# Attention of a decoder layer: queries normalised, turned and projected one quarter earlier, and stacked ahead of the keys

## The chip, the cores and the metric

The kernel runs on one core of one Trainium2 chip, as a single launch. The metric is the device time of that launch in microseconds (us). The engines are named as in the profile: PE is TensorE (PEld its weight loads), DVE is VectorE, ACT is ScalarE, POOL is GpSimd, SP is SyncE, which here only issues DMAs (SPq is its queue).

## What is computed

One decoder layer on x of shape (32, 100, 256), in fp32: a recurrent token mixer, a cross attention of 16 heads against a context of 361 keys with 192 channels, and a mixture of 8 experts of which 2 are taken per token. The change touches the second stage alone:

```python
    def _L0_xattn_ref(query, key_value, Wq, bq, Wk, bk, Wv, bv, Wo, bo):
        q = (query @ Wq + bq).reshape(B, Nq, H, D).transpose(0, 2, 1, 3)
        k = (key_value @ Wk + bk).reshape(B, Nkv, H, D).transpose(0, 2, 1, 3)
        v = (key_value @ Wv + bv).reshape(B, Nkv, H, D).transpose(0, 2, 1, 3)
        attn = jnp.einsum('bhqd,bhkd->bhqk', q, k) * scale
        attn = jnp.clip(attn, -CLAMP, CLAMP)
        attn = jax.nn.softmax(attn, axis=-1)
        x = jnp.einsum('bhqk,bhkd->bqhd', attn, v).reshape(B, Nq, Cq)
        return x @ Wo + bo
    x = x + _L0_attn_ref(_layernorm(x, axis=-1), ...)
    x = x + _L0_xattn_ref(_layernorm(x, axis=-1), ctx_768, ...)
    x = x + _L0_ffn_ref(_layernorm(x, axis=-1), ...)
```

## The kernel before

The three stages run one after the other: the mixer, the attention, the experts. Every engine has its own program, written out by hand, and runs it strictly in that order; semaphores tie the programs together. Nothing reorders them.

**The loop of the attention.** `every_batch` writes out 32 bodies, one for each batch b. A body has four quarters t = 0 to 3; a quarter handles four of the 16 heads. In quarter t PE computes, in this order: half of the scores of the next quarter (`scores`, L1551, into `bank_s`), the transposed scores of this quarter in three pieces (`scores_t`, L1561, into `bank_st`), the weighted sum of the quarter before (`weigh`, L1581), the other half of the next quarter's scores, and last `shift` (L1570), which subtracts each row's maximum by a matmul with a diagonal of maxima. The scores of the next batch's first quarter are thus computed in quarter 3: this is where PE first needs the next batch's queries and keys.

**Around it.** DVE takes the maxima of `bank_s` (L1357), writes them negated (L1362), and clips `bank_st` (L1368). POOL builds the diagonal from the maxima (`diag`, L1086, tile `neg_diag`); `shift` of quarter t waits for `diag` of quarter t. ACT takes the exponentials after `shift` (`exps`, L1231).

**Queries and keys.** The scores are taken in bf16 with each fp32 number split in three parts. ACT rounds to the high part (L1210 for a half of the keys, L1225 for all queries), and POOL computes the middle and the low part (`split_k`, L1067 to L1071, once for each half; `split_q`, L1076 to L1080). SP then copies the parts of 16 channels each into `k_st` and `q_st`, six slots of 16 partitions on top of each other (`stack`, L965): 12 DMAs for the keys and 12 for the queries of a batch, waiting for each part before its copies. `k_st` and `q_st` hold three batches.

The queries of batch b + 2 are prepared in body b: POOL computes the norm's factors (`norm`, L1047 to L1051), ACT applies them in quarter 1 (L1264), PE turns the result at the end of quarter 2 (`turn`, L1522), ACT copies it (`turned`, L1214), PE projects it at the end of quarter 3 (`queries`, L1529), and ACT adds the bias and rounds (L1221, L1225). The keys of b + 2 are projected in quarters 2 and 3 (L1514). POOL splits the second half of the keys and the queries at the start of body b + 1, ahead of that body's `diag` of quarter 1.

**What POOL does besides.** In even bodies from b = 4 on it also sends the routed rows of two earlier batches to HBM (`tag`, `count_on`, and four indirect DMAs, `send`, L1133: two ahead of `diag(b, 3)`, one behind it, one ahead of `diag(b + 1, 0)`). In odd bodies it has `route_pair` (L1094 to L1104) ahead of `diag(b, 3)`. `norm3` (L1056 to L1060) belongs to the third stage's layer norm; ACT's `row` (L1272) and PE's turn of it (L1610, in quarter 0) wait for it.

## Time and profile before

| | us |
|---|---|
| median of 3 runs | 1618.37 |
| lowest, highest | 1614.95, 1623.78 |
| profiled execution, its own time | 1619.98 |
| its span in the trace | 1618.1 |

The trace covers the profiled execution; 1.9 us lie around its span. The mixer takes the first 494 us, the attention runs from there to about 1249 us, and the experts from then on. The attention's loop starts at 526.0 us with the first scores and takes its batches at 22.3 us each. The profile shows for each engine its instructions in order of time, how long it sat idle before one, and what ended that idle time (the releaser, behind "<-"). [...]

### The profile page before, as it was taken

The page shows a single profiled execution, that of the slowest core. Times are in us where ns is not written, and L with a number is a line of the kernel's source. Part 1 is how long each engine was busy: PE and PEld are TensorE (multiplying, and loading weights), DVE is VectorE, ACT ScalarE, POOL GpSimd, SP SyncE. Part 2 cuts the span into 40 slices and gives each one's busy share as a digit, 9 for nine tenths or more (in the row PEclk, how much of TensorE's full clock was granted, in tenths as well). Part 3 has the DMA queues.
Part 4 walks back from the last instruction along what each step waited for, and adds up shares of the span by engine and source line. Part 5 has one row for each costly group of instructions (what it writes and reads, how often), then busy time and mean ns, then how long its engine had stood idle before and what let it go on. Part 6 is the DMA issues. An engine that isn't in the chain of part 4 may idle for free. (4 is left out here: it accounts for less than half of the span.)

```text
span 1618.1 us, 31781 instructions
## 1 busy us (share of the span) xinstructions
PE 1365.9 (84%) x9914; PEld 916.8 (57%) x9915; DVE 988.9 (61%) x2297; ACT 578.7 (36%) x1420; POOL 801.1 (50%) x1138
## 2 busy tenths in 40 slices
PE   4788778778746899988898888998886699999996
PEld 2455555545534566666666666666653366666664
DVE  2687987797740777877777777787875122222221
ACT  1333323323312455554444545445543121222221
POOL 4234642463343557776676676776764122222222
PEclk9899999999965999999999999999996799999999
DMA  4991000000004655555555565655551132222222
GB/s 147 322 321 39 1 1 1 0 0 1 1 0 79 92 92 111 118 111 106 111 106 113 107 111 88 116 116 110 112 100 53 40 46 46 46 45 44 44 46 23
DMA packets 180331, 128.03 MB, mean 79 GB/s; under 512 B 69010, under 2 KB 173090, under 8 KB 180194
## 3 DMA queue, kind: packets, MB, share of 16 engines
q1 hardware_dynamic: 167890, 112.23, 32.8%
q0 software_dynamic: 12304, 14.10, 5.8%
q8 instruction: 70, 1.15, 0.4%
q14 instruction: 67, 0.55, 0.1%
HBM read 36.10 MB, written 44.83 MB: 50 GB/s over the span
## 5 line engine op out<-in xcount | busy, mean ns | idle before, releaser
L1357 DVE TENSOR_REDUCE neg_raw<-bank_s 100x2 f32<-100x722 f32 x256 | 230.8, 902 | 95.0 <-PE bank_s L1551 82.8
L1231 ACT ACTIVATE prob<-bank_st 120x400 f32<-120x400 f32 (+1 forms) x384 | 166.4, 513 | 220.3 <-PE bank_st L1570 213.6
L1892 POOL DMA_INDIRECT out<-result,target x57 | 88.2, 1547 | 266.9 <-DVE result L1866 263.9
L1368 DVE TENSOR_SCALAR bank_st<-bank_st 120x400 f32<-120x400 f32 (+1 forms) x384 | 196.6, 573 | 0.0
L751 PE MATMUL bank_l<-q_heads,k 128*100 128x192 f32 (+4 forms) x512 | 126.9, 390 | 62.0 <-DVE attn L565 49.9
L1551 PE MATMUL bank_s<-k_st,q_st 96*128 96x361 bf16 x512 | 129.7, 336 | 56.5 <-DMA q_st<-q_part 53.7
L1877 DVE TENSOR_TENSOR hidden<-silu,ebank_v 128x512 f32<-128x512 f32 x57 | 39.2, 688 | 196.9 <-PE ebank_v L1801 196.9
L751 PEld LDWEIGHTS bank_l<-q_heads,k 128*100 128x100 f32 x512 | 82.8, 180 | 113.0 <-DVE attn L565 43.5
L399 ACT ACTIVATE q_heads<-q 32x192 f32<-32x192 f32 (+3 forms) x168 | 62.1, 369 | 226.3 <-DVE q L524 220.7
L1086 POOL TENSOR_TENSOR neg_diag<-xident_b,neg_max 100x400 bf16<-100x400 bf16 x128 | 109.3, 854 | 60.4 <-DVE neg_max L1362 57.4
L1514 PE MATMUL bank_m<-kv,xw_k 96*128 96x361 f32 x256 | 107.8, 551 | 10.9 <-DMA kv<-in_ctx_t 10.2
L1801 PE MATMUL ebank_g<-expert_w,rows_t 128*128 x228 | 109.9, 605 | 1.2 <-DVE rows_t L1857 0.8
L275 POOL TENSOR_TENSOR mixed<-part,xn_t 128x400 f32<-128x400 f32 x80 | 78.9, 1012 | 63.5 <-DVE part L441 63.5
L1561 PE MATMUL bank_st<-q_st,k_st 96*128 96x100 bf16 x1536 | 105.2, 211 | 4.2 <-ACT prob L1231 0.3
L1820 PE MATMUL ebank_y<-residual,hidden_t 128*128 x456 | 108.0, 380 | 0.9 <-ACT hidden_t L1848 0.9
L1801 PE MATMUL ebank_v<-expert_w,rows_t 128*128 x228 | 108.0, 596 | 0.0
L1561 PEld LDWEIGHTS bank_st<-q_st,k_st 96*128 96x128 bf16 x1536 | 84.6, 100 | 38.1 <-ACT prob L1231 25.4
L1848 ACT ACTIVATE hidden_t<-ebank_h 128x512 f32<-128x512 f32 x57 | 34.0, 597 | 198.1 <-PE ebank_h L1811 198.1
L1539 PE MATMUL bank_v<-xw_v,kv 96*120 96x256 f32 (+1 forms) x384 | 98.5, 394 | 1.4 <-ACT xval L1249 0.7
L1581 PE MATMUL bank_o<-prob,xval 120*32 120x100 f32 (+1 forms) x3072 | 98.1, 263 | 0.5 <-ACT prob L1231 0.5
L281 POOL TENSOR_TENSOR gn_rstd<-gn_mv,eps 100x16 f32<-100x16 f32 x8 | 2.4, 300 | 183.6 <-DVE gn_mv L578 183.6
L1570 PE MATMUL bank_st<-neg_diag,xones_b 100*128 100x400 bf16 x384 | 89.9, 342 | 2.2 <-POOL neg_diag L1086 1.8
(207 smaller groups left out, 2734.0 us busy)
## 6 DMA issues: line engine op xcount, KB each, us to landing
k_st<-k_part SPq DMA_DIRECT2D x384, 90.2 KB
slot_rows<-empty SPq DMA_DIRECT2D x9, 2967.0 KB, 26.0
q_st<-q_part SPq DMA_DIRECT2D x384, 25.0 KB
kv<-in_ctx_t SPq DMA_DIRECT2D x32, 270.8 KB
expert_w<-in_w SPq DMA_DIRECT2D x16, 512.0 KB, 3.9
rows<-slot_rows SPq DMA_DIRECT2D x57, 129.0 KB
residual<-in_w SPq DMA_DIRECT2D x16, 256.0 KB, 4.4
residual<-in_x SPq DMA_DIRECT2D x8, 400.0 KB
```

The source lines that it names most:

```text
L751: pe.matmul(bank[0:T, at:at + RH * cols], k[:, p, j, 0:T], q_heads[:, lv % 2, :, j, 0:cols], start=True, stop=True).then_inc(level_summed, 1)
L1086: pool.tensor_tensor(neg_diag[:, t % 2], ident_b[:].unsqueeze(1).to_broadcast([T, 4, T]), neg_max[:, 4 * t:4 * t + 4].unsqueeze(2).to_broa ...
L1231: act.activation(prob[0:KEYS[c], t % 2, c], bank_st[c][0:KEYS[c], 0:4 * T], ACT.Exp).then_inc(exp_done, 1)
L1357: dve.tensor_reduce(neg_raw[:, h:h + 2], bank_s[0:T, :, 0:S], AX.X, ALU.max, negate=True).then_inc(max_done, 1)
L1368: dve.tensor_scalar(tile, tile, CLAMP, -CLAMP, ALU.min, ALU.max).then_inc(clipped, 1)
L1514: mm = pe.matmul(bank_m[:, 0:S], w_k[:, i, c * 128:(c + 1) * 128], kv[:, p, i], start=(i == 0), stop=(i == 1))
L1539: mm = pe.matmul(bank_v[0:KEYS[c], (c % 2) * D:(c % 2 + 1) * D], kv[:, p, i, KEY0[c]:KEY0[c] + KEYS[c]], w_v[:, i], start=(i == 0), stop=( ...
L1551: mm = pe.matmul(bank_s[0:WIDE, i, 0:S], q_st[:, r, h * T:h * T + WIDE], k_st[:, r, h * S:(h + 1) * S], start=True, stop=True)
L1561: mm = pe.matmul(bank_st[c][0:WIDE, j * T:(j + 1) * T], k_st[:, r, at:at + WIDE], q_st[:, r, h * T:(h + 1) * T], start=(j == 0), stop=Fals ...
L1581: mm = pe.matmul(bank_o[32 * j:32 * j + 32, t * T:(t + 1) * T], val[0:KEYS[c], p, c, 17 * (4 * t + j):17 * (4 * t + j) + 32], prob[0:KEYS[ ...
L1801: mm = pe.matmul(dst[:], rows_t[:, u, c], w1_of[:, bass.ds(expert, 1), c, half * F:(half + 1) * F].rearrange("p o f -> p (o f)"), start=(c ...
L1820: mm = pe.matmul(bank_y[:, 0:D], hidden_t[:, u, f], w2_of[:, bass.ds(expert, 1), f].rearrange("p o d -> p (o d)"), start=(f == 0), stop=(f ...
```

## The change

In the steady bodies of the attention the chain that prepares the queries of batch b + 2 moves one quarter forward on every engine, and SP copies the queries of a batch before its keys. The instructions and their shapes are the same, and so is their number.

```diff
@@ stack(b, r), on SP
                 until(st_summed, 12 * (b - 2))
                 until(s_summed, 8 * (b - 2))
-                for c in range(CC):
-                    until(k_high, CC * b + c + 1)
-                    spread(k_st, k_part, (0, 2, 5), 0, c, k_stacked)
-                    until(k_mid, CC * b + c + 1)
-                    spread(k_st, k_part, (1, 4), 1, c, k_stacked)
-                    until(k_low, CC * b + c + 1)
-                    spread(k_st, k_part, (3,), 2, c, k_stacked)
                 until(q_high, b + 1)
...
                     spread(q_st, q_part, (5,), 2, c, q_stacked)
+                for c in range(CC):
+                    until(k_high, CC * b + c + 1)
+                    spread(k_st, k_part, (0, 2, 5), 0, c, k_stacked)
+                    until(k_mid, CC * b + c + 1)
+                    spread(k_st, k_part, (1, 4), 1, c, k_stacked)
+                    until(k_low, CC * b + c + 1)
+                    spread(k_st, k_part, (3,), 2, c, k_stacked)
@@ body, on POOL
+                if more_than(b, 2):
+                    norm(b + 2)
                 if more_than(b, 1):
                     split_k(b + 1, 1)
-                    split_q(b + 1)
+                if b == 0:
+                    split_q(1)
                 diag(b, 1)
-                if more_than(b, 2):
-                    norm(b + 2)
@@
                 diag(b, 3)
+                if more_than(b, 2):
+                    split_q(b + 2)
                 if sends:
                     send(h, hp, 1, 0)
@@ body, on ACT
                     exps(4 * b + t, t)
                     if t == 1 and more_than(b, 2):
-                        norm(b + 2)
+                        turned(b + 2)
...
+                    if t == 0 and more_than(b, 2):
+                        norm(b + 2)
                     if more_than(b, 2) and t >= 2:
                         keys(b + 2, t - 2)
                     if more_than(b, 2) and t == 2:
-                        turned(b + 2)
-                    if more_than(b, 2) and t == 3:
                         queries(b + 2)
@@ body, on PE
+                    if more2 and t == 1:
+                        turn(b + 2)
                     if more2 and t == 2:
-                        turn(b + 2)
-                    if more2 and t == 3:
                         queries(b + 2)
```

**POOL, an even body with sends.** From the send behind `diag(b, 3)` to `diag(b + 1, 0)`, before:

```order
L1133 DMA slot_rows<-row,slots 26496x258
L1056 TENSOR_TENSOR moment<-moment,xeps 100x1
L1058 TENSOR_TENSOR moment<-moment,xpower 100x1
L1060 TENSOR_SCALAR moment<-moment 100x1
L1067 TENSOR_TENSOR kr<-kf,k_part 128x361
L1068 TENSOR_TENSOR k_part<-kf,k_part 128x361
L1071 TENSOR_TENSOR k_part<-kr,k_part 128x361
L1133 DMA slot_rows<-row,slots 26496x258
L1086 TENSOR_TENSOR neg_diag<-xident_b,neg_max 100x400
```

and with the change:

```order
L1076 TENSOR_TENSOR qr<-qf,q_part 128x200
L1077 TENSOR_TENSOR q_part<-qf,q_part 128x200
L1080 TENSOR_TENSOR q_part<-qr,q_part 128x200
L1133 DMA slot_rows<-row,slots 26496x258
L1056 TENSOR_TENSOR moment<-moment,xeps 100x1
L1058 TENSOR_TENSOR moment<-moment,xpower 100x1
L1060 TENSOR_SCALAR moment<-moment 100x1
L1067 TENSOR_TENSOR kr<-kf,k_part 128x361
L1068 TENSOR_TENSOR k_part<-kf,k_part 128x361
L1071 TENSOR_TENSOR k_part<-kr,k_part 128x361
L1133 DMA slot_rows<-row,slots 26496x258
L1086 TENSOR_TENSOR neg_diag<-xident_b,neg_max 100x400
```

The three operations of `split_q` moved from behind `diag(b + 1, 0)` to well ahead of it, and they wait there for ACT's rounded queries.

**PE, from the end of quarter 2 to the start of the next body's quarter 0.** Before:

```order
L1570 MATMUL bank_st<-neg_diag,xones_b 128x400 x3
L1522 MATMUL bank_v<-xident,xxn 128x100 x2
L1551 MATMUL bank_s<-k_st,q_st 128x361 x2
L1561 MATMUL bank_st<-q_st,k_st 128x100 x12
L1581 MATMUL bank_o<-prob,xval 32x100 x12
L1551 MATMUL bank_s<-k_st,q_st 128x361 x2
L1514 MATMUL bank_m<-kv,xw_k 128x361 x2
L1570 MATMUL bank_st<-neg_diag,xones_b 128x400 x3
L1529 MATMUL bank_v<-xxn_t,xw_q 128x100 x4
L1551 MATMUL bank_s<-k_st,q_st 128x361 x2
L1561 MATMUL bank_st<-q_st,k_st 128x100 x12
```

and with the change (its lines stand 3 further down in the file):

```order
L1573 MATMUL bank_st<-neg_diag,xones_b 128x400 x3
L1532 MATMUL bank_v<-xxn_t,xw_q 128x100 x4
L1554 MATMUL bank_s<-k_st,q_st 128x361 x2
L1564 MATMUL bank_st<-q_st,k_st 128x100 x12
L1584 MATMUL bank_o<-prob,xval 32x100 x12
L1554 MATMUL bank_s<-k_st,q_st 128x361 x2
L1517 MATMUL bank_m<-kv,xw_k 128x361 x2
L1573 MATMUL bank_st<-neg_diag,xones_b 128x400 x3
L1554 MATMUL bank_s<-k_st,q_st 128x361 x2
L1564 MATMUL bank_st<-q_st,k_st 128x100 x12
```

The projection of the queries now stands ahead of the next batch's first scores, and nothing stands any more between `shift` of quarter 3 and the next body.

## Rows read from the trace of the kernel before

**Rows 1.** Who waited for whom: engine, line, releaser: total us, times, longest.

```profile
PE bank_s L1551 <- DMA q_st<-q_part: 53.7, 30, 2.9
PE bank_st L1570 <- POOL neg_diag L1086: 1.8, 1, 1.8
```

**Rows 2.** Busy time by stretch: bounds, length, engines' busy us, clock, DMA, GB/s.

```profile
608.30:1187.98 579.68, 516.88 (x5721) 365.57 (x5722) 440.83 (x949) 293.73 (x796) 413.47 (x693) 0.96 0.57 109
...
807.80:813.90 6.10, 6.04 (x55) 4.09 (x56) 4.62 (x9) 1.76 (x6) 5.35 (x9) 0.72 0.46 117
```

**Rows 3.** PE's timeline, even body 16: start, us, line, operation [idle before <-releaser].

```profile
896.42 0.67 PE L1570 MATMUL bank_st<-neg_diag,xones_b 100*128 100x400 bf16 x3
...
898.66 0.47 PE L1551 MATMUL bank_s<-k_st,q_st 96*128 96x361 bf16 x2 [1.39 <-DMA q_st<-q_part]
...
902.29 1.03 PE L1529 MATMUL bank_v<-xxn_t,xw_q 128*128 128x100 f32 x8
...
907.21 0.67 PE L1570 MATMUL bank_st<-neg_diag,xones_b 100*128 100x400 bf16 x3
```

**Rows 4.** PE's timeline, quarter 3 of even body 12, released after a wait.

```profile
807.86 0.47 PE L1551 MATMUL bank_s<-k_st,q_st 96*128 96x361 bf16 x2 [1.47 <-DMA q_st<-q_part]
...
813.13 1.03 PE L1529 MATMUL bank_v<-xxn_t,xw_q 128*128 128x100 f32 x8
```

**Rows 5.** SP's queue: the 12 copies of a batch's queries, in two bodies.

```profile
798.32 7.65 SPq L965 DMA_DIRECT2D q_st<-q_part  x12
...
820.50 8.54 SPq L965 DMA_DIRECT2D q_st<-q_part  x12
```

**Rows 6.** ACT's timeline in the same even body: quarter 2 behind the exponentials, then quarter 3.

```profile
898.51 0.58 ACT L1204 ACTIVATE kf<-bank_m,xb_k 128x361 f32<-128x361 f32 x1
898.96 0.36 ACT L1214 ACTIVATE xxn_t<-bank_v 128x200 f32<-128x200 f32 x1
...
904.26 0.59 ACT L1221 ACTIVATE qf<-bank_v,xb_q 128x100 f32<-128x100 f32 x2
904.89 0.37 ACT L1225 ACTIVATE q_part<-qf 128x200 bf16<-128x200 f32 x1
```

**Rows 7.** POOL's timeline around the same body, splitting queries and sending rows.

```profile
887.08 0.56 POOL L1076 TENSOR_TENSOR qr<-qf,q_part 128x200 f32<-128x200 f32 x1
...
888.83 0.86 POOL L1086 TENSOR_TENSOR neg_diag<-xident_b,neg_max 100x400 bf16<-100x400 bf16 x1
...
898.45 0.85 POOL L1086 TENSOR_TENSOR neg_diag<-xident_b,neg_max 100x400 bf16<-100x400 bf16 x1 [1.88 <-DVE neg_max L1362]
...
905.74 0.86 POOL L1086 TENSOR_TENSOR neg_diag<-xident_b,neg_max 100x400 bf16<-100x400 bf16 x1
```

**Rows 8.** PE's timeline, odd body 13's quarter 3 to even body 14's quarter 2.

```profile
830.69 0.47 PE L1551 MATMUL bank_s<-k_st,q_st 96*128 96x361 bf16 x2 [2.15 <-DMA q_st<-q_part]
831.00 0.70 PE L1561 MATMUL bank_st<-q_st,k_st 96*128 96x100 bf16 x12
...
834.33 1.03 PE L1529 MATMUL bank_v<-xxn_t,xw_q 128*128 128x100 f32 x8
835.20 0.47 PE L1551 MATMUL bank_s<-k_st,q_st 96*128 96x361 bf16 x2
...
839.89 0.67 PE L1570 MATMUL bank_st<-neg_diag,xones_b 100*128 100x400 bf16 x3
...
849.75 0.67 PE L1570 MATMUL bank_st<-neg_diag,xones_b 100*128 100x400 bf16 x3
```

**Rows 9.** PE's timeline, body 0: transposed scores with little ahead of them.

```profile
544.03 1.08 PE L1561 MATMUL bank_st<-q_st,k_st 96*128 96x100 bf16 x12
```

**Rows 10.** The loop's start: ACT's first rounded queries, PE's first scores.

```profile
512.20 0.37 ACT L1225 ACTIVATE q_part<-qf 128x200 bf16<-128x200 f32 x1
...
525.98 0.47 PE L1551 MATMUL bank_s<-k_st,q_st 96*128 96x361 bf16 x2
```

**Rows 11.** PE's timeline, body 30: the loop's last wait for a stack.

```profile
1210.73 0.47 PE L1551 MATMUL bank_s<-k_st,q_st 96*128 96x361 bf16 x2 [2.04 <-DMA q_st<-q_part]
```

## The prediction, made before the change was run

> **What bounds the kernel now.** I read the table of waits first. PE waits 30 times, 53.7 us in all, for a landing of queries ahead of L1551 [rows 1]: once a body, at the start of quarter 3, where the next batch's first scores begin. Next, the busy time by stretch: over 26 bodies PE is busy 516.9 of 579.7 us (89%), POOL 413.5 (71%), DVE 440.8 (76%) [rows 2]. A body takes 579.7 / 26 = 22.3 us, a pair of an even and an odd body 44.6 us; 26 bodies x 1.8 us of this wait are most of PE's idle time. Last, the timelines around the wait. [...]
>
> The wait is SP's. Twelve copies take 7.65 us to issue even when nothing holds them up [rows 5], 0.64 us each; the last ends at 805.97 and PE is released at 807.86 [rows 4], 1.9 us later.
>
> **The change, step by step.** All times are counted from the start of `shift` of quarter 2, S.
>
> SP. The high parts of the queries now open the stack. Behind the exponentials of quarter 2 the keys' bias starts at S + 2.09 (898.51 - 896.42) [rows 3, 6], the next operation 0.45 after that (898.96); the queries' bias and rounding take 0.63 (904.26 to 904.89) + 0.37 [rows 6]. So the high parts are ready at S + 3.55. 24 copies at 0.64 are 15.3 us; in another body 12 took 8.54 instead of 7.65 [rows 5], so I add 0.9; with 1.9 for landing all is there at S + 21.7. PE wants it one body later at S' + 1.4 (the two start-ups of `shift`, 0.51, and of the projection, 0.87, from 834.33 to 835.20 [rows 8]). With a body of 20.3 us or more the wait at quarter 3 is gone. SP no longer pauses between the pieces, since each part is ready before it is asked for. The landing of the larger last piece (keys, 90 KB against 25 KB) is seen in no row; I take the queries' 1.9 us, from 1.9 to 3.1 for the range. [...]
>
> PE. The projection (0.87) leaves quarter 3 and the turn (0.34) quarter 2; they stand one quarter earlier. Their work is unchanged, but the projection was cover: behind `shift` of quarter 3 the transposed scores must now wait for ACT's exponentials. Where only the turn stood there, the 12 took 1.08 instead of 0.70 us (544.03 against 831.00) [rows 8, 9]; with nothing there I take 0.5 us, from 0.4 to 0.9.
>
> POOL is where I expect the gain to be lost. In an even body with sends, it goes from the end of the diagonal of quarter 3 (898.45 + 0.85 = 899.30) to the start of the next body's first diagonal (905.74) without a pause: a send, `norm3`, `split_k`, a send, 6.44 us [rows 7]. PE uses that diagonal at 907.21, 0.6 us after its end [rows 3, 7]. There is hardly slack even now. The change puts `split_q` ahead of all of it, 1.75 us (887.08 to 888.83) [rows 7], and it has to wait until S + 3.55 for ACT, 0.65 us after POOL came free. The diagonal then ends at 3.6 + 1.75 + 6.44 + 0.86 = S + 12.7. PE would like to have it at 1.4 (its scores begin) + 3.63 (quarter 3 without the projection, 898.66 to 902.29) + 0.5 + 4.05 (907.21 - 902.29 - 0.87) [rows 3] = S + 9.6. **A new wait of 3.1 us for `neg_diag` in every second body.** Until now PE waited for it once in the whole run, 1.8 us [rows 1]. Behind the waiting `shift` stand the routing, the next scores and, on ACT, the exponentials; nothing of them can pass.
>
> The odd body: no sends, but `diag` of quarter 3 stands behind `route_pair`. Its own end is late, yet 1.75 + about 1.2 + 2.7 + 0.85 us later PE is only about at its `shift`: from S it needs 0.51 + 0.87 + 3.64 + 0.5 + 4.69 (835.20 to 839.89) = 10.2 us [rows 8]. I count no wait there, 0.5 at the most.
>
> The sum for a pair. From the even body's S to the odd body's first `shift`: 12.7 us (before: 907.21 - 896.42 = 10.8 in this body [rows 3]; with a low stretch in it 12.3). From first `shift` to S inside a body: 9.86 (839.89 to 849.75) [rows 8] + 0.34 for the turn = 10.2, twice. From the odd body's S to the next first `shift`: 10.2. Together 43.3 us, against 44.6: 1.3 us less a pair, at the upper clock throughout. Thirteen pairs have sends: -16.9 us.
>
> The clock. Before, the low stretches came behind waits of 1.4 to 2.9 us, behind some and not others (807.86 yes, 830.69 no, by the time that quarter 3 took [rows 4, 8]), roughly once a pair. The new wait is longer but comes half as often. I take a low stretch behind every second one: 6.5 x 1.6 = +10.4. The bounds are 0 and 13 x 1.6 = +20.8. [...]
>
> The ends. At the start the first copies of keys no longer run ahead: SP begins with the queries at 512.6 [rows 10], issues 24 copies in 15.7 us and PE begins at about 530.1 instead of 525.98: +4.1. Bodies 1 to 3 have no sends, so their waits really go (about 1.2 a body and a low stretch): -4.7. Body 30 has no `split_q`, so its wait of 2.04 us [rows 11] goes and a low stretch with it (1.6), less 1.1 of new stalls behind exponentials: -2.5. These three make -3.1.
>
> Sum: -16.9 + 10.4 - 3.1 = -9.6 us. The profiled execution took 1620.0, so it would take 1610.4; it lies 1.6 above the median, and the forecast is 1618.4 - 9.6 = **1609 us**.
>
> **The rivals.**
> *No wait for POOL.* If the sends or the splits give way and PE gets its diagonal in time, a body is bounded by PE and the stack, 20.4 to 20.8 us: 26 x 1.8 = 47 us less, 1570 us. [...] Against it: the 6.44 us without a pause [rows 7]. 10%.
> *The clock falls behind every new wait.* The gain of 1.3 is less than the 1.6 of a low stretch: 13 x 0.3 = +4, less 3.1: 1619 us. 20%.
> *Slower.* The wait for `neg_diag` is so long that a low stretch lasts twice as long (3.2 us). It decides from 1.3 us of low-clock loss per pair on; 13 x (3.2 - 1.3) - 3 = +22: 1640 us. For it: PE idles 3.1 us within 9, longer than any wait now (2.9 [rows 1]). Against it: by then the next bodies have slack again. 12%.
> *The change doesn't do what it says:* the last keys land as late as the queries did, because SP's queue still ends late; the same wait under another name beside POOL's: 1622 us. Against it are the pauses that SP loses. 8%.
>
> **How the numbers follow.** My forecast, a wait for POOL with the clock falling behind some of its waits, has 50%, with 1599 to 1617 as its own range (clock bounds, 12.5 to 12.9 for POOL's chain, 0.4 to 0.9 for ACT's). A measurement of this kernel tells about 0.5%, 8 us, from no change: below 1610.3 faster, above 1626.5 slower. Faster takes 0.34 of my forecast and the first rival: 0.44. Slower: the third rival and a little of the rest, 0.14. Same: 0.42. The range reaches over the second and fourth rival and leaves out the first and most of the third: 1589 to 1631.
>
> **What would show it.** Right: the wait for `q_st` at L1554 nearly gone from the table; a new entry of PE for `neg_diag` (L1573 for L1086) of 25 to 45 us in 12 to 14 waits, all at quarter 0 of odd bodies; SP copying without pauses; transposed scores at 1.1 instead of 0.7 us in quarter 0; the first scores at about 530 us. Wrong: waits for `k_st` at quarter 3 (SP is the bound), no wait for `neg_diag` (POOL had room), or ACT's `row` (L1273) reached so late that PE stops at its turn (L1613) for more than a microsecond. The clock's share, 0.96 over the 26 bodies now [rows 2], tells the rivals apart: 0.97 or more gives the lower end of the forecast, 0.95 or less the slower case.

## The result and the profile after

The changed kernel takes 1663.35 us (median of 4 runs, 1651.83 to 1670.75), the kernel before beside it 1617.84 (4 runs). The ratio is 1.027, with a 95% interval of 1.0193 to 1.0347. The forecast was 1609, the range 1589 to 1631: the kernel became slower, and by more than any of the rivals allowed (1640 at the most). One execution of a kernel of the experiments (e5) took 2315.28 us at a granted clock of 0.556, and no median or ratio below counts it.

The profiled execution is the slowest of the four (1670.75 us). The first lines of its page, and the granted clock by slices:

```profile
span 1668.9 us, 31781 instructions
## 1 busy us (share of the span) xinstructions
PE 1406.0 (84%) x9914; PEld 937.4 (56%) x9915; DVE 984.4 (59%) x2297; ACT 591.1 (35%) x1420; POOL 800.8 (48%) x1138
...
PEclk9899999999775898997899889989998699999999
```

The same 26 bodies as in [rows 2], the busy time by stretch, first after, then before. The stretch runs from the first scores of batch 4, in quarter 3 of body 3, to those of batch 30. The columns are the bounds, the length, the busy time of PE, PEld, DVE, ACT and POOL (instructions), the granted clock, the share of the DMA engines and GB/s:

```profile
627.05:1237.86 610.81, 554.15 (x5722) 385.43 (x5721) 436.48 (x950) 304.15 (x794) 412.33 (x689) 0.91 0.65 102
```

```profile
608.32:1187.94 579.62, 516.84 (x5720) 365.51 (x5721) 440.83 (x949) 293.71 (x796) 413.43 (x692) 0.96 0.57 109
```

The two spans differ by 1668.9 - 1618.1 = 50.8 us. The bounds of these lines split it: bodies 4 to 29, counted so, begin 627.05 - 608.32 = **18.7** us later, take 610.8 - 579.6 = **31.2** longer, and what follows takes 431.0 instead of 430.2, **0.9** more.

The 31.2 us are no idle time. PE's idle time in the stretch went from 579.62 - 516.84 = 62.8 to 610.81 - 554.15 = 56.7 us: down by 6.1. Its busy time, for the same 5720 matmuls, went up by 37.3. The clock column gives the reason, 0.91 instead of 0.96.
```profile
903.84:907.26 3.42, 3.37 (x33) 2.48 (x33) 3.13 (x7) 0.39 (x1) 3.01 (x4) 0.50 1.14 120
920.90:927.73 6.83, 6.83 (x43) 4.92 (x44) 4.01 (x8) 1.52 (x5) 6.37 (x11) 0.50 0.31 66
```

Where the waits went, from the table of waits (engine, line, releaser: total us, times, longest):

```profile
PE bank_s L1554 <- DMA k_st<-k_part: 24.3, 8, 8.0
PE bank_st L1573 <- POOL neg_diag L1086: 21.7, 14, 1.8
PE bank_m L1627 <- ACT kf L1207: 14.0, 14, 1.1
PE bank_m L1613 <- ACT kf L1207: 8.5, 10, 0.9
```

Before, behind the start, PE waited for `kf` only at `count`:

```profile
PE bank_m L1624 <- ACT kf L1204: 4.9, 14, 0.4
```

The 53.7 us for `q_st` of [rows 1] are gone. There came the wait for `neg_diag` that was foretold (13 of the 14 stand in odd bodies; the one in body 31 was there before), and one that was named only as a sign of being wrong: PE waits for ACT's `kf` (the keys' bias, counted by `k_done`), in even bodies at `count` (L1627; 4.9 us in 14 before), in odd ones at `turn3` (L1613; none before). Both, in PE's timeline of odd body 15 and even body 16 (start, us, line, operation, idle time before it and releaser):

```profile
889.55 0.67 PE L1573 MATMUL bank_st<-neg_diag,xones_b 100*128 100x400 bf16 x3
...
895.00 1.15 PE L1564 MATMUL bank_st<-q_st,k_st 96*128 96x100 bf16 x12
...
898.11 0.36 PE L1613 MATMUL bank_m<-xident,row 100*128 100x100 f32 x2 [0.90 <-ACT kf L1207]
898.31 1.91 PE L1542 MATMUL bank_v<-xw_v,kv 96*121 96x256 f32 x8
901.77 0.68 PE L1573 MATMUL bank_st<-neg_diag,xones_b 100*128 100x400 bf16 x3 [1.55 <-POOL neg_diag L1086]
...
904.89 1.23 PE L1584 MATMUL bank_o<-prob,xval 121*32 121x100 f32 x24
...
920.82 0.41 PE L1627 MATMUL bank_m<-pairs,before 100*100 100x16 f32 x2 [1.05 <-ACT kf L1207]
...
923.56 3.66 PE L1542 MATMUL bank_v<-xw_v,kv 96*121 96x256 f32 x8
```

In one pair PE stops three times, 0.90, 1.55 and 1.05 us, where before it stopped twice for the stack. Behind the last two the clock fell: the 24 matmuls of L1584 take 1.23 us at 904.89 (0.72 at the upper clock, as in e9's rows below), and the values of L1542 3.66 at 923.56 instead of 1.91 at 898.31.

POOL's timeline from quarter 3 of even body 14 to that odd body's first diagonal shows why `neg_diag` is late, and why `kf` is:

```profile
890.38 0.85 POOL L1086 TENSOR_TENSOR neg_diag<-xident_b,neg_max 100x400 bf16<-100x400 bf16 x1 [1.60 <-DVE neg_max L1365]
892.61 0.56 POOL L1076 TENSOR_TENSOR qr<-qf,q_part 128x200 f32<-128x200 f32 x1 [1.38 <-ACT q_part L1228]
...
896.62 0.26 POOL L1060 TENSOR_SCALAR moment<-moment 100x1 f32<-100x1 f32 x1
...
900.86 0.86 POOL L1086 TENSOR_TENSOR neg_diag<-xident_b,neg_max 100x400 bf16<-100x400 bf16 x1
```

From the `shift` of quarter 2 at 889.55, POOL waits for the rounded queries until 3.06 us, and the next diagonal ends at 901.72, 12.17 us; the forecast said 12.7. `norm3` (`moment`) now stands behind the split. Its result releases ACT's `row`, and `kf` stands behind `row` on ACT.

The start. SP's queue, then ACT's timeline, then PE's:

```profile
512.11 7.80 SPq L965 DMA_DIRECT2D q_st<-q_part  x12
520.43 7.71 SPq L965 DMA_DIRECT2D k_st<-k_part  x12
...
535.53 10.88 SPq L965 DMA_DIRECT2D q_st<-q_part  x12
546.53 8.99 SPq L965 DMA_DIRECT2D k_st<-k_part  x12
```

```profile
533.09 0.51 ACT L1213 ACTIVATE k_part<-kf 128x361 bf16<-128x361 f32 x1 [11.60 <-DMA k_st<-k_part]
```

```profile
533.05 0.78 PE L1554 MATMUL bank_s<-k_st,q_st 96*128 96x361 bf16 x2 [7.62 <-DMA k_st<-k_part]
...
560.32 0.78 PE L1554 MATMUL bank_s<-k_st,q_st 96*128 96x361 bf16 x2 [8.02 <-DMA k_st<-k_part]
```

The first scores come at 533.05, 7.1 us later than in [rows 10] (4.1 were expected). Worse is body 0. `k_part` is one buffer: by the program ACT may round the keys of batch 1 only when all key copies of batch 0 have landed, and these now go last. So ACT stands 11.60 us, the queries of batch 1, which stand behind on ACT, are rounded after it, and SP begins the second stack at 535.53. Quarter 3 of body 0 waits 8.02 us for it.

Landing. SP issued the last key copy of the first stack at 520.43 + 7.71 = 528.14, and PE was released at 533.05, 4.9 us later. The forecast took 1.9. The busy time by stretch in bodies 11 and 12 (columns as above; the last but one is the DMA engines' share, which counts a transfer where it starts and so can pass 1), first while SP issues twelve key copies, then from the last issue to PE's scores:

```profile
805.99:813.72 7.73, 7.05 (x62) 5.05 (x63) 4.33 (x11) 3.40 (x10) 6.29 (x11) 0.78 0.96 120
813.72:818.98 5.26, 5.26 (x61) 3.95 (x60) 4.28 (x9) 2.10 (x6) 0.00 (x0) 1.00 1.16 157
```

Before, over the query copies of [rows 5] at 820.50:

```profile
820.50:829.03 8.53, 7.77 (x91) 5.11 (x88) 7.20 (x16) 3.49 (x10) 3.98 (x8) 1.00 0.49 53
```

Twelve key copies in a row keep the DMA engines at a share of 0.96, and at 1.16 for 5 us after SP has done: they are issued as fast as they are moved, and a backlog remains. Wherever PE waited for `k_st` in this kernel and those below whose key copies go last, it was released 3.0 to 6.5 us after SP's last copy, mostly 4 to 6 (without a wait its scores began as early as 2.7 us after it); before, behind the queries' copies, PE was released after 1.5 to 2.1. There SP paused between the pieces of the keys (11.63 to 12.20 us for twelve copies, at 808.75 and 786.01, against 7.73 here), and the small copies of the queries ended the stack at a share of 0.49.

### The profile page after: what moved, and what is told of

Read it like the earlier page. It is cut to its first block and busy times, and to the rows that moved or that the text cites. A ratio compares the mean times of both kernels' runs of the same rounds, so it can differ in the third digit from the quotient of the medians.

```text
span 1668.9 us, 31781 instructions
## 1 busy us (share of the span) xinstructions
PE 1406.0 (84%) x9914; PEld 937.4 (56%) x9915; DVE 984.4 (59%) x2297; ACT 591.1 (35%) x1420; POOL 800.8 (48%) x1138
## 3 DMA queue, kind: packets, MB, share of 16 engines
q8 instruction: 70, 1.15, 0.3%
## 5 line engine op out<-in xcount | busy, mean ns | idle before, releaser
L1554 PE MATMUL bank_s<-k_st,q_st 96*128 96x361 bf16 x512 | 134.1, 346 | 27.7 <-DMA k_st<-k_part 24.3
L1542 PE MATMUL bank_v<-xw_v,kv 96*120 96x256 f32 (+1 forms) x384 | 120.9, 462 | 1.4 <-ACT xval L1252 0.8
L1564 PE MATMUL bank_st<-q_st,k_st 96*128 96x100 bf16 x1536 | 113.4, 215 | 4.7 <-ACT prob L1234 0.7
L1573 PE MATMUL bank_st<-neg_diag,xones_b 100*128 100x400 bf16 x384 | 91.4, 345 | 22.5 <-POOL neg_diag L1086 21.7
L1584 PE MATMUL bank_o<-prob,xval 120*32 120x100 f32 (+1 forms) x3072 | 105.0, 276 | 0.5 <-ACT prob L1234 0.5
L1517 PE MATMUL bank_m<-kv,xw_k 96*128 96x361 f32 x256 | 95.4, 497 | 11.0 <-DMA kv<-in_ctx_t 10.3
L1542 PEld LDWEIGHTS bank_v<-xw_v,kv 96*120 96x120 f32 (+1 forms) x384 | 85.9, 234 | 20.2 <-issue 2.1
```

Of the source, the lines that this page charges most:

```text
L1517: mm = pe.matmul(bank_m[:, 0:S], w_k[:, i, c * 128:(c + 1) * 128], kv[:, p, i], start=(i == 0), stop=(i == 1))
L1542: mm = pe.matmul(bank_v[0:KEYS[c], (c % 2) * D:(c % 2 + 1) * D], kv[:, p, i, KEY0[c]:KEY0[c] + KEYS[c]], w_v[:, i], start=(i == 0), stop=( ...
L1554: mm = pe.matmul(bank_s[0:WIDE, i, 0:S], q_st[:, r, h * T:h * T + WIDE], k_st[:, r, h * S:(h + 1) * S], start=True, stop=True)
L1564: mm = pe.matmul(bank_st[c][0:WIDE, j * T:(j + 1) * T], k_st[:, r, at:at + WIDE], q_st[:, r, h * T:(h + 1) * T], start=(j == 0), stop=Fals ...
L1584: mm = pe.matmul(bank_o[32 * j:32 * j + 32, t * T:(t + 1) * T], val[0:KEYS[c], p, c, 17 * (4 * t + j):17 * (4 * t + j) + 32], prob[0:KEYS[ ...
```

## The experiments

Each kernel ran beside the kernel before, three rounds and more. "26 bodies" is bodies 4 to 29, counted as above, in the profiled execution, "low" the time at a clock of 0.50 in them, "stack" PE's waits ahead of the first scores of a batch in the whole run (total us and times). A wait that the table of waits puts down to "issue" at the same line is counted with it. The other two columns are PE's waits for `neg_diag`, and for `kf` at `count` and `turn3` together.

| kernel | median us | ratio (95%) | 26 bodies | low | neg_diag | kf | stack |
|---|---|---|---|---|---|---|---|
| before | | 1 | 579.6 | 51 | 1.8, 1 | 4.9, 14 | 53.9, 31 |
| changed | 1663.4 | 1.027 (1.019-1.035) | 610.8 | 116 | 21.7, 14 | 22.5, 24 | 24.3, 8 |
| e1 start, keys first | 1638.6 | 1.015 (1.007-1.022) | 592.9 | 68 | 15.9, 11 | 17.7, 20 | 23.7, 15 |
| e2 keys first in all stacks | 1667.8 | 1.033 (1.026-1.040) | 620.9 | 89 | 20.2, 13 | 15.4, 22 | 41.7, 23 |
| e3 small split | 1650.5 | 1.017 (1.014-1.021) | 594.3 | 82 | 14.4, 10 | 10.2, 19 | 37.3, 17 |
| e4 filler | 1652.8 | 1.023 (1.017-1.028) | 588.3 | 38 | 4.9, 8 | 13.7, 17 | 45.1, 23 |
| e6 norm3 first | 1649.8 | 1.017 (1.015-1.020) | 598.7 | 82 | 17.1, 13 | 8.7, 13 | 43.4, 17 |
| e7 mixed stack | 1636.8 | 1.009 (1.006-1.012) | 609.6 | 113 | 22.1, 14 | 26.1, 27 | 1.3, 3 |
| e8 = e7 + e6 | 1605.0 | 0.989 (0.985-0.993) | 572.0 | 61 | 20.3, 13 | 9.4, 14 | 5.1, 4 |
| e9 = e8 + filler | **1589.2** | 0.985 (0.980-0.990) | 554.5 | 14 | 6.3, 13 | 9.4, 14 | 3.8, 4 |
| e11 = e9, keys last | 1637.3 | 1.010 (1.007-1.014) | 594.4 | 52 | 5.7, 11 | 8.0, 12 | 36.9, 18 |
| e5 before + 24 fillers | 1604.3 | 0.993 (0.990-0.996) | 565.0 | 14 | 1.8, 1 | 4.9, 14 | 29.7, 29 |
| e10 before + 12 | 1610.0 | 0.998 (0.995-1.001) | 566.4 | 24 | 1.8, 1 | 4.6, 13 | 41.2, 30 |
| e10 before + 40 | 1606.0 | 0.994 (0.991-0.996) | 568.5 | 3 | 1.8, 1 | 4.9, 14 | 17.7, 20 |

A profile is one execution, and the executions of one kernel differ: those of the kernel before ran from 1607.5 us at a mean clock of 0.939 to 1625.3 at 0.930 in one row of rounds, and its medians beside the experiments from 1616.6 to 1621.0. So the sums of waits explain, and the medians decide. The profiled executions of e2, e4, e5, e9 and both e10 were the fastest of their kernels, those of the changed kernel, e6, e7 and e8 the slowest; a difference of 26 bodies between such two overstates the medians' by 10 us or so.

**The start: e1.** In the changed kernel, the stacks of batches 0 and 1 are led by the keys again; all later ones are unchanged.

```diff
+                if b < 2:
+                    stack_keys()
+                    stack_queries()
+                else:
+                    stack_queries()
+                    stack_keys()
```

> The changed kernel, but the stacks of batches 0 and 1 copy their keys ahead of their queries, as before the change; all later stacks copy the queries first. Theory A (one third of the loss is made once, at the start: with the queries first the keys of batch 0 land late, ACT may not overwrite their high part before that, and the queries of batch 1 behind it are late too): first scores of batch 1 in quarter 3 at about 544 to 546 us instead of 560.3, the whole 14 to 18 us faster than the changed kernel, about 1647 us. Rival B (the start is made good later, by slack in the steady bodies): within 4 us of the changed kernel, about 1663 us.

Measured: 1638.63 us, 24.7 less than the changed kernel, more than the 14 to 18 expected. Its first scores came at 525.29, and quarter 3 of body 0 came 18.5 us after them (27.3 in the changed kernel, 17.7 before). The first scores of batch 4 come at 613.6 instead of 627.05, 13.4 us earlier. That is the start's share, shown: the order of the first two stacks alone. The other 11 us lie in the steady bodies, which the edit doesn't touch; low time was 68 instead of 116 us. Why less is not shown; part of it is the spread of the runs.

**The order of the stack in the steady state: e2.** The changed kernel with the keys ahead of the queries in every stack, as before. It separates SP's order from the moves on the compute engines.

```diff
+                for c in range(CC):
+                    until(k_high, CC * b + c + 1)
+                    spread(k_st, k_part, (0, 2, 5), 0, c, k_stacked)
...
                 until(q_high, b + 1)
...
                     spread(q_st, q_part, (5,), 2, c, q_stacked)
-                for c in range(CC):
-                    until(k_high, CC * b + c + 1)
-                    spread(k_st, k_part, (0, 2, 5), 0, c, k_stacked)
...
```

> The changed kernel with SP's order of before in all stacks: keys, then queries. PE, ACT and POOL stay as changed. Theory A (the order on SP costs only at the start; in the steady bodies the loss is on POOL, on ACT and in PE's clock): the start's 16 us come back, but the wait for the queries at quarter 3 returns, about 1 to 2 us a body, beside the wait for neg_diag; 1655 to 1690 us. Rival B (the order on SP is what costs in the steady bodies too): back to 1615 to 1630 us.

Measured: 1667.79 us, as slow as the changed kernel, although the start is mended here too (first scores of batch 4 at 605.7), and 29 us slower than e1, from which it differs only in the stacks from batch 2 on. The 26 bodies are the longest of all, 620.9, and PE stands at quarter 3 again (a wait ahead of L1554 that the table puts down to "issue"):

```profile
PE bank_s L1554 <- issue: 40.2, 22, 3.3
...
PE bank_st L1573 <- POOL neg_diag L1086: 20.2, 13, 1.8
```

So queries first is the right order for the moved chain. What the change loses in the steady bodies is not undone by SP's old order.

**POOL's chain: e3 and e6.** e3 does the three operations of `split_q` on 4 of 100 columns, so that the middle and low parts of the other columns are left out (they stay zero); the first is shown, the other two are cut alike. e6 puts `norm3` ahead of `split_q`.

```diff
-                pool.tensor_tensor(qr[:], qf[:], q_part[:, 0], ALU.subtract).then_inc(q_rest, 1)
+                pool.tensor_tensor(qr[:, :, 0:4], qf[:, :, 0:4], q_part[:, 0, :, 0:4], ALU.subtract).then_inc(q_rest, 1)
```

> The changed kernel with the three POOL operations that split the queries done on 4 of 100 columns, so the middle and low parts of the other columns of the queries are left out (filled with zero once at the start) and the output differs. Everything else, the copies, the waits and their order, is unchanged. POOL's work behind the diagonal of quarter 3 shrinks by about 1.2 to 1.5 of its 1.75 us. Theory 1 (POOL's chain and what ACT waits for behind it set the new stalls): PE's waits for neg_diag (21.7 us in 14, in the changed kernel) fall to under 8 us, those for ACT's kf (14.0 in 14) to under 7, low stretches from 24 to under 17, the 26 bodies from 610.8 to 585-597 us, the time from 1663 to 1635-1650. Waits for k_st at quarter 3 grow, as in the runs with shorter bodies, since the key copies end 5 to 6 us after SP's last issue. Rival (the new waits of PE don't matter, the stack of copies bounds the body): time and 26 bodies stay within 5 us of the changed kernel, the waits move to k_st.

```diff
                 diag(b, 3)
+                if not (isinstance(b, int) and b == 0):
+                    norm3(b - 1)
                 if more_than(b, 2):
                     split_q(b + 2)
                 if sends:
                     send(h, hp, 1, 0)
-                if not (isinstance(b, int) and b == 0):
-                    norm3(b - 1)
```

> The changed kernel with norm3 ahead of the split of the queries on POOL instead of behind it. ACT's row, and through it the keys' bias (kf) that PE waits for, come 1.75 us or more earlier; the length of POOL's chain up to the next diagonal is the same, but POOL no longer waits for ACT's rounding at its start (1.6 us in 16 waits). Theory 1: PE's waits for kf (14.0 us in 14) are nearly gone, those for neg_diag (21.7) fall to 8-18 since the 0.65 us pause of POOL ahead of the split goes; low stretches 24 to 14-20, 26 bodies 592-602, time 1640-1652. Rival (kf's waits of 1 us cost nothing by themselves, only the wait for neg_diag does): 26 bodies 603-612, time 1652-1664.

Measured: 1650.48 and 1649.80 us, each about 13 less than the changed kernel. The totals lie where theory 1 put them (e3 half a microsecond above its upper end; the intervals of the ratios just overlap that of the changed kernel), and so does e6's wait for `neg_diag`. Two numbers were missed. In e3 the wait for `neg_diag` fell only to 14.4 us, not under 8: POOL still waits for ACT's rounding (1.25 us) ahead of a split that is now 0.6 us long, so from `shift` of quarter 2 to the end of the next diagonal it takes 11.4 instead of 12.2 us. And the waits for `kf`: those at `turn3` went (0.8 us in e3, none in e6, of 8.5), but at `count` 9.4 and 8.7 of 14.0 us stayed, where e6 was to leave nearly nothing. What was taken away came back in part as waits for the stack, 37.3 and 43.4 us in 17.

**Landing: e7, e11.** e7 starts with e1's order and, from batch 2 on, copies the queries' high parts, then the keys, then the queries' middle and low parts. SP's 24 copies are the same; only the last ones are now small.

```diff
+                else:
+                    stack_high()
+                    stack_keys()
+                stack_rest()
```

> The changed kernel with the stacks of batches 0 and 1 led by the keys (as in e1_start_keys_first, 1638.6 us), and in the stacks of all later batches the order: high parts of the queries, keys, middle and low parts of the queries. So the last copies of a stack are 25 KB instead of 90 KB. Theory 1 (the key copies come faster than the DMA engines move them: DMA share 0.97 while twelve are issued and 1.16 in the 5 us after, so they land 5 to 6 us after SP's last issue; the queries' copies behind them use that time): PE's waits at quarter 3 for a stack go from 23.7 us (15) to under 10 us, the time from SP's last copy to PE's first scores can be as short as 2 to 3 us (least value over the bodies; 3.5 in e1_start_keys_first), and the total is 1625-1637. Rival (the landing is not what bounds those bodies, or the queries' copies queue behind the keys' all the same): the same waits under q_st's name, 1637-1650.

Measured: 1636.80 us. PE's waits for the stack are gone (1.3 us in 3), and the shortest time from SP's last copy to PE's scores is 1.54 us, where it was 3.6 in e1 from batch 2 on. So the order of the copies sets this time: with 90 KB copies at the end PE is released 3.0 to 6.5 us after SP's last, with 25 KB copies behind them as early as 1.5. How long the keys themselves took to land in e7 it does not tell: SP issues six small copies after the last one of the keys. But the time is the upper end of what was expected, and that of e1 within its spread: with the waits for `neg_diag` and `kf` as in the changed kernel (22.1 and 26.1 us), the bodies only wait elsewhere. The landing alone doesn't bound the changed kernel, whose other stops are as late.

e8 adds e6's edit to e7.

> e7_mix with norm3 ahead of the split of the queries on POOL, as in e6_norm3_first. The middle and low parts of the queries are now asked for 10 us later, so POOL's later split holds up nothing. Theory 1 (start, landing, the late kf and POOL's pause are the four causes, and they add): 1605-1625 us, PE's waits for kf nearly gone, for neg_diag under 15 us, for the stack under 10. Rival (the loop through POOL and ACT stays as long and the low-clock stretches follow whatever wait is left): 1625-1645.

Measured: 1604.98 us, faster than the kernel before (0.989, 0.985 to 0.993). The two together gain 32 us over e7, where e6 alone gained 13: with keys last, the shorter chain ran into the landing. The time is the lower end of what was expected. The wait for `neg_diag` stayed at 20.3 us, over the 15 expected, and that for `kf` at 9.4, where nearly nothing was. But the stops for `kf` at `count` are 0.67 us instead of 1.05, and the low stretches behind them 7 with 24 us instead of 10 with 65 in e7. The clock still falls 18 times in the 26 bodies.

**The clock: e4, e9, e5, e10.** e4 is the changed kernel with 24 matmuls ahead of the first `shift` of the odd bodies from 5 on, into a corner of a bank that nobody reads. They wait for nothing that is late (in e9's rows none of them stands behind a wait), so PE works through the wait for `neg_diag`.

```diff
+            def fill(n):
+                for _ in range(n):
+                    pe.matmul(bank_o[0:128, 4 * T:5 * T], ones_b[:], ident_b[:], start=True, stop=True)
...
+                    if t == 0 and p == 1 and b >= 5:
+                        pe.wait_ge(ot_done, b)
+                        fill(24)
                     for c in range(3):
                         shift(n, t, c)
```

> The changed kernel with 24 more matmuls on PE (bf16, 100 columns, about 1.25 us at the upper clock, results used by nobody) ahead of the shift of quarter 0 in odd bodies from 5 on, where PE waits 1.5 to 1.8 us for neg_diag. They lengthen no chain. Theory A (the steady loss is the clock: PE sits idle there and its clock falls afterwards): fewer low stretches, their sum between 545 and 1215 us down from 133 us to 90 or less, 15 to 35 us faster than the changed kernel, about 1638 us. Rival B (the loss is the waits themselves and the low clock comes from elsewhere): the same sum of low stretches and 1660 to 1668 us.

Measured: 1652.84 us, 10.5 less, with more work done. That is less than the 15 to 35 expected, yet outside the rival's 1660 to 1668; the ratios, 1.023 and 1.027, have overlapping intervals, so by the times alone this gain is not clear of the noise. Low time in the profile is 38 instead of 116 us, and the 26 bodies are 22.5 us shorter, not 39, which is half of the low time saved. The stack's waits rose from 24.3 to 45.1 us in 23: behind the clock stands the landing.

e9 is e8 with the same filler.

> e8_mix_norm3 (1605.0 us; in its trace PE waits 20.3 us in 13 for neg_diag, and one low stretch of 3.4 us follows in nearly every body of 22.24 us) with 24 matmuls whose result nobody reads ahead of the first shift of the odd bodies from 5 on, where that wait is. 24 of them take 1.2 us, less than the wait of 1.4 to 1.8. Theory (the clock term: PE's idle time ahead of that shift is what the low stretches follow): low stretches between the start and the tail fall from 19 to under 10, the 26 bodies from 572.0 to 555-565 us, the time to 1588-1600. Rival (the low stretches follow other waits of the body, those of 0.3 to 0.7 us for ACT, or the loop through POOL sets the body whatever the clock): 26 bodies 568-576, time within 5 us of e8_mix_norm3.

Measured: **1589.20 us**, ratio 0.985, the fastest of all, 15.8 less than e8 (its expectation held). The executions of the two do not overlap (1586.7 to 1594.1 against 1596.9 to 1612.7); set against the kernel before beside each, the step is smaller, 0.985 against 0.989, with overlapping intervals. The wait for `neg_diag` in the odd bodies is now work, and the clock holds:

```profile
843.79 1.91 PE L1552 MATMUL bank_v<-xw_v,kv 96*121 96x256 f32 x8
845.53 1.23 PE L1582 MATMUL bank_o<-xident_b,xones_b 100*128 100x100 bf16 x24
846.60 0.67 PE L1588 MATMUL bank_st<-neg_diag,xones_b 100*128 100x400 bf16 x3
...
849.26 0.72 PE L1599 MATMUL bank_o<-prob,xval 121*32 121x100 f32 x24
```

```profile
601.78:1156.27 554.49, 526.17 (x6034) 369.46 (x6033) 444.43 (x950) 302.54 (x794) 411.30 (x689) 0.99 0.71 114
```

PE does 312 matmuls more than in the changed kernel and is busy 28 us less, at a clock of 0.99 instead of 0.91.

e11 takes one thing back from e9: keys last, as in the change.

> e9_mix_norm3_fill (1589.2 us) with one thing undone: from batch 2 on the keys are copied last again, as in the changed kernel, behind all parts of the queries. Nothing else differs. Theory (the landing of the key copies, 3.5 to 6 us after SP's last issue, bounds a body once it is short): from the first scores of quarter 3 to the high parts 2.15 us, 16.3 us for 24 copies, 3.5 to 6 us of landing make 22 to 24.4 us a body, so the 26 bodies take 572-590 us instead of 554.5, PE waits for k_st at quarter 3 15 to 25 times, 25-50 us in all, and the total is 1603-1622. Rival (with the waits for POOL covered, the order of the stack no longer matters): 26 bodies 553-565, total within 6 us of 1589.

```profile
PE bank_s L1562 <- DMA k_st<-k_part: 36.9, 18, 3.9
```

Measured: 1637.32 us, 48.1 more than e9. The theory's waits came (36.9 us in 18), the loss was larger than its 1603 to 1622: the profile has 52 us of low time again, in spite of the fillers at POOL's wait. PE now stands uncovered at quarter 3, up to 3.9 us, and all 8 low stretches of the 26 bodies begin in or behind such a wait. A wait for a copy costs its own length and, at 8 of the 15 that were longer than 0.6 us, a low stretch.

e5 and e10 put the filler into the kernel before, ahead of the first scores of quarter 3, where PE waits for `q_st`.

```diff
+                    if t == 3 and 1 <= b < BATCH - 1:
+                        fill(24)
                     if go:
                         scores(nb, nb % 3, nt, 0)
```

> The kernel before with the same 24 matmuls ahead of the first scores of quarter 3 in bodies 1 to 30, where PE waits 1.8 us on average for the queries. Theory A (idle time of this size is what makes the clock fall): the 61 us at the lower clock between 545 and 1215 us go to 20 or less; 15 low stretches of 1.6 us are about 24 us, so about 1595 to 1603 us. Rival B (the clock does not follow this wait): 1615 to 1630 us, since a few waits are shorter than the filling.

> The kernel before with 12 instead of 24 unread matmuls ahead of the first scores of quarter 3 (24 gave a ratio of 0.9928, 4 low stretches instead of 15). 12 take 0.6 us of a wait of 1.5 to 2.9. If the low clock follows the length of PE's idle time, half the cover leaves 8 to 12 stretches and a ratio of 0.993 to 1.000. Rival (any cover will do): 4 to 6 stretches, ratio 0.990 to 0.995.

> The kernel before with 40 unread matmuls there, 2.0 us, about the whole wait. The stack's loop through SP sets the body then, not PE: 26 bodies 562-568 us (565.0 with 24), 2 to 6 low stretches, ratio 0.990 to 0.996. Rival (the matmuls now delay the scores and the delay adds up, since PE is the bound): 26 bodies 572 or more, ratio 0.998 or more.

Measured: ratios of 0.993 with 24 (0.990 to 0.996), 0.998 with 12 (0.995 to 1.001, which includes 1) and 0.994 with 40 (0.991 to 0.996). With 24 the clock held as the first theory said, but the time, 1604.3, is above its 1595 to 1603: low time fell by 37 us in the 26 bodies, and they became 14.6 us shorter, where half of 37 is 18.5. Twelve fillers lie within the first theory's 0.993 to 1.000, though the profile's low stretches were fewer than it said (6 in the 26 bodies, 13 without fillers). With 40 there is one low stretch left and nothing more is gained; that SP's loop then sets the body, as expected, was not tested (PE still waits 17.7 us ahead of the scores). So of the kernel before, about 12 us (0.7%) hung on PE standing idle 1.8 us on average, 2.9 at the most, once a body.

## Why the prediction was wrong

**Right.** The wait for `q_st` is gone. The wait for `neg_diag` has its place, quarter 0 of odd bodies, and its count, 13 (and the old one of body 31). POOL's chain was sized well: 12.2 us in nearly every odd body, 12.7 forecast. The wait itself was half as long as forecast, 1.55 us against 3.1 (21.7 in all, 25 to 45 forecast): besides the half microsecond of POOL, PE comes later, at S + 10.7 instead of 9.6, because it has stood 0.90 us for `kf` at `turn3` by then. The transposed scores take 1.15 us in quarter 0 (895.00), 1.1 forecast. The pair of 43.3 us "at the upper clock throughout" is borne out only by estimates: take half of the low time away, and the changed kernel's pair is (610.8 - 58) / 13 = 42.5, and that of e4, where less is taken away, (588.3 - 19) / 13 = 43.8. The gain of 16.9 us stood on it. That it can be had shows in e9, at a clock of 0.99, with a pair of 554.5 / 13 = 42.7; but e9 has another order on SP and POOL too. The changed kernel doesn't reach it.

**Wrong: the clock, +10.4 forecast, about +58 found.** This is the term that turned the sign. The 58 us are half of the 116 at a clock of 0.50, an estimate that is exact only while PE is the engine that the others wait for (less came back in e4, 22.5 us of 39, and in e5, 14.6 of 18.5). Measured directly, PE's busy time for the same matmuls rose by 37.3 us; by the forecast's 10.4, against half of the 51 us before (25.6), it should have fallen by about 15. "A low stretch behind every second new wait, 1.6 us each" made 6.5 stretches for the 26 bodies. The trace has 22. Behind the foretold wait stand 11, not 6.5, with 44 us; half of that is 22, about the upper bound of 20.8. The other 11, with 72 us, half of it 36, stand behind the stop for `kf` at `count`, for which the sum had nothing.

Both factors failed. The count, because the forecast looked at one wait a pair and took PE's other stops as harmless; the clock fell behind stops of 1 us as well (1.05 at 920.82). The price, because 1.6 us is read from one low stretch behind one wait: from PE's release to the projection 813.13 - 807.86 = 5.27 us in [rows 4], where the clock was 0.68 on average, and 834.33 - 830.69 = 3.64 in [rows 8], at a clock of 1.00. No run shows this price for the stretches of the changed kernel: they last 4.0 us on average behind `neg_diag` and 6.5 behind `kf`. Why they last longer there is not shown; no further stop of PE over 0.25 us lies in them. The third rival, low stretches twice as long, came nearest with 1640, but still with a stretch only at POOL's wait. The forecast's own sign for the slower case, a clock of 0.95 or less over the 26 bodies, came true with 0.91. That PE's idle time is what the clock follows is shown by e5, with 24 and with 40 fillers (14 and 3 us at 0.50 in the 26 bodies, 51 without), and by e9 against e8 (14 against 61), and e4's trace agrees (38 against 116): filled with useless work, it leaves the clock up, and the kernel gets faster (in e4 by less than the noise can tell).

**Wrong: the second wait, not in the sum.** `split_q` was followed to the diagonal behind it, not to `norm3`, which it also delays. From `moment` to ACT's `row` to `kf` to PE is a chain of its own, 1 us late in both bodies of a pair, 22.5 us in all against 4.9 before, and the costlier half of the low time stands behind it (above). The forecast listed it as a sign of being wrong and gave it no price. e6, which only lets `norm3` go first, gains 13.6 us; it shortens POOL's chain a little as well (11.0 us instead of 12.2), so that not all of it is the price of `kf`.

**Wrong: the landing, 1.9 us (1.9 to 3.1) forecast, 3.0 to 6.5 found.** The queries' 1.9 us was the time of a small copy at the end of a queue with the DMA engines at a share of 0.49. The twelve copies of 90 KB that now close the stack come at 0.64 us each without a pause, and the DMA engines fall behind (a share of 0.96, then 1.16). The step "with a body of 20.3 us or more the wait is gone" should have said 21.5 to 25 (24 copies 16.3 us, 3.0 to 6.5 for landing, 2.15 from PE's scores to the next high parts). In the changed kernel, whose bodies are 23.5 us, this costs little; it takes back part of what e1, e3, e4 and e6 gain, and e11 against e9 prices it at 48 us with the clock's share.

**Wrong: the start, 4.1 - 4.7 = about -0.6 forecast, +18.7 found.** The first scores were 3 us later than forecast, by the landing again. The rest is the reuse of `k_part`: the forecast followed each copy to its reader and not to the writer of its source's next content. That ACT could not round the keys of batch 1, and so, in order, the queries behind, was to be read from the code and in no row of before, where the keys' copies were done by then. e1 takes both away together and gets 13.4 us of it back; that the larger part is the reuse is read from ACT's row and the program. Bodies 1 to 3, which were to give 4.7 back, took 66.7 us instead of 64.6.

The end (body 30) was to give 2.5 and gave nothing; from the first scores of batch 30 to the end it took 0.9 us more. The wait of 2.04 us for batch 31 is gone, but in body 30 too PE stops 1.06 us for `kf`, with 10.2 us at a clock of 0.50 behind it, and the first scores of batch 31 come 24.3 us after those of batch 30, before 22.8.

## What to carry to other kernels

Price an engine's idle time together with what its clock does behind it: here a pair of bodies with three stops of about 1 us (47.0 us long) cost more than one with two stops of about 2 (44.6), and the cure of a wait is worth its low stretch as well. When an operation is moved ahead of others on an in-order queue, follow every consumer of all that stands behind it, not only the next one; and when a copy is moved back, ask who may overwrite its source, above all where there is one buffer. Put the small transfers last in a group that someone waits for: here a reader was released 1.5 us after the last small copy, and 3.0 to 6.5 after the last of twelve large ones. And where PE's idle time falls but the time doesn't, compare its busy time for the same instructions: here the loss stood there, 37.3 us.

## What the runs showed of the hardware

- Useless matmuls in PE's waits made the kernel faster: 24 of them, 1.2 us, in place of a wait of 1.3 to 1.9 us brought 15.8 us between the medians of e8 and e9, and the granted clock over the 26 bodies went from 0.95 to 0.99. In the kernel before they gave a ratio of 0.993. In the changed kernel the clock went from 0.91 to 0.97 and the median down by 10.5 us (e4, intervals overlapping).
- The clock fell to 0.50 behind stops of only about 1 us (11 of 13 at `count` in the changed kernel), in e8 and e9 even behind some of 0.67 us (7 and 4 of 13). The trace of the changed kernel has 22 low stretches in 26 bodies, 116 us in all.
- Whether the last copies of a stack are 90 KB or 25 KB moved the time from SP's last issue to their reader from 3.6 to 1.5 us at the least (e1, e7), at a DMA share of 0.96 to 1.16 for the former in the changed kernel. Where PE waited for `k_st` with twelve key copies last in the stack, it was released 3.0 to 6.5 us after SP's last copy.
